# Two token blocks ahead in layer 1's expert stage, and a reordered passage between the layers

## The reference

```python
x = x + tanh(g_xattn) * cross_attention(layernorm(x), ctx)   # 16 heads of 16
x = x + tanh(g_ffn)   * mixture_of_experts(layernorm(x))     # 8 experts, top 2
```

## Time and profile before

| | us |
|---|---|
| median of 3 runs | 691.21 (691.18 to 691.99) |
| the profiled execution | 698.34 |
| its span, first to last instruction | 696.5 |
| PE busy in the span | 641.9 (92%) |
| DVE, ACT, POOL busy | 386.9, 336.9, 268.3 |
| first block of layer 1 starts on PE | 578.85 |
| first and last full block's first product, and first half block's, start | 578.85, 648.02, 650.28 |

### The profile page before, as it was taken

The page is one execution under the profiler, slowest core; times in us unless marked ns, Lnnn a source line. Parts: engine busy times, 40 slices in busy tenths (PEclk is TensorE's granted clock), DMA queues, the critical chain, the costliest instruction groups (busy, mean ns, idle before and its releaser), DMA issues.

```text
span 696.5 us, 18912 instructions
## 1 busy us (share of the span) xinstructions
PE 641.9 (92%) x6536; PEld 506.7 (73%) x6536; DVE 386.9 (56%) x1262; ACT 336.9 (48%) x675; POOL 268.3 (39%) x501
## 2 busy tenths in 40 slices
PE   8899999899999999999999999879999999989960
PEld 5667777667999999999995555557777766768630
DVE  3778899864443322232223222568999896744317
ACT  4566566442455455545531112458777643434420
POOL 5662555533232121112111111214477555866540
PEclk9999999999999999999999999999999999999995
DMA  9144555651123111111115000611122135454219
GB/s 230 38 151 140 165 193 171 207 185 47 62 85 92 39 32 39 36 35 33 39 54 132 32 17 16 209 50 33 62 72 70 63 109 138 148 161 124 81 58 357
DMA packets 50478, 69.74 MB, mean 100 GB/s; under 512 B 7751, under 2 KB 37831, under 8 KB 50387
## 3 DMA queue, kind: packets, MB, share of 16 engines
q1 hardware_dynamic: 41276, 49.66, 23.1%
q0 software_dynamic: 6528, 17.90, 7.2%
q10 hardware_dynamic: 2583, 0.98, 0.6%
HBM read 46.28 MB, written 22.23 MB: 98 GB/s over the span
## 4 chain that ended last, share of the span: by engine, by line
PE 71%; DVE 14%; issue 5%; DMA 5%; POOL 2%; ACT 1%; SPq 1%; another core or an unknown queue 1%; DVEq 0%; POOLq 0%; ACTq 0%
PE ps L1993 17%; PE ps L2049 17%; PE ps L1977 12%; DVE m_rows L1179 4%; PE ps L1763 4%; PE ps L1718 3%; PE ps L1701 3%; PE ps L1755 3%; PE ps L1801 2%; DVE x_sb L1163 2%; PE ps L1777 2%; PE ps L1729 1%; DVE ctx_q L1196 1%; DMA xs_dram<-xn,slot_now 1%; PE ps L2025 1%
## 5 line engine op out<-in xcount | busy, mean ns | idle before, releaser
L2049 PE MATMUL ps<-w_all,share 128*128 (+3 forms) x576 | 137.6, 382 | 3.3 <-ACT w_all L1062 2.1
L718 POOL DMA_INDIRECT ys_dram<-share,dest_i x36 | 37.6, 1044 | 204.1 <-DVE share L1538 203.8
L2049 PEld LDWEIGHTS ps<-w_all,share 128*128 128x128 f32 (+3 forms) x576 | 97.5, 179 | 22.6 <-issue 6.7
L1977 PE MATMUL ps<-w_all,share 128*128 (+1 forms) x336 | 97.5, 430 | 3.8 <-DVE share L1325 3.3
L686 POOL DMA_INDIRECT xs_dram<-xn,slot_now x64 | 66.3, 1036 | 68.0 <-PE ps L1764 15.5
L1993 PEld LDWEIGHTS ps<-share,w_att 128*128 128x128 f32 x768 | 89.4, 192 | 1.3
L1993 PE MATMUL ps<-share,w_att 128*128 128x128 f32 x768 | 89.6, 275 | 0.0
L1977 PEld LDWEIGHTS ps<-w_all,share 128*128 128x128 f32 (+1 forms) x336 | 53.2, 166 | 36.9 <-issue 10.4
L1179 DVE TENSOR_REDUCE m_rows<-ps 128x8 f32<-128x960 f32 x64 | 70.5, 1142 | 12.0 <-PE ps L1718 11.8
L1322 DVE SCALAR_TENSOR_TENSOR xid<-share,be 128x1 f32<-128x1 f32 x36 | 7.8, 217 | 74.8 <-PE ps L1801 60.1
L1011 ACT ACTIVATE share<-ps 128x512 f32<-128x512 f32 x24 | 14.3, 598 | 69.4 <-PE ps L1993 69.4
(11 more groups left out here) (266 smaller groups left out, 1326.0 us busy)
## 6 DMA issues: line engine op xcount, KB each, us to landing
w_all<-ys_dram SPq DMA_DIRECT2D x16, 512.0 KB, 7.1
w_all<-gate SPq DMA_DIRECT2D x8, 688.0 KB
w_all<-up SPq DMA_DIRECT2D x8, 688.0 KB
w_all<-down SPq DMA_DIRECT2D x8, 640.0 KB
w_all<-w SPq DMA_DIRECT2D x16, 256.0 KB
share<-xs_dram SPq DMA_DIRECT2D x28, 129.0 KB
w_all<-xs_dram SPq DMA_DIRECT2D x28, 129.0 KB
out<-x_sb SPq DMA_DIRECT2D x8, 256.0 KB, 5.5
```

Of the source, the lines that this page charges most:

```text
L718: g.indirect_dma_start(ys_dram, bass.IndirectOffsetOnAxis(ap=dest_i[:, w:w + 1], axis=0), block_y(l, j), None).then_inc(stored(l, j)[0], 16)
L1977: i = t.matmul(ps[0:r, bank, 0:w], xgT[:, k, 0:r], w_all[:, bass.ds(off + (k * UPW[l] + col - EW[l]), w)], start=(k == 0), stop=(k == KT - 1))
L2049: i = t.matmul(ps[0:n, 6, 0:D], h[:, 0:n], w_all[0:r, bass.ds(off + (KT * UPW[l] + c * D - EW[l]), D)], start=(c == 0), stop=(c == KD[l] - 1))
```

## The change

1. **Columns two blocks ahead in layer 1.** A second buffer `xgT_odd`; even and odd blocks alternate. At step j PE transposes block j+2 and DVE copies it out, except at step 0 and at steps 11 to 16, where it stays one ahead (`next_blocks`, `REJOIN` = 17). Steps 1 and 17 take two blocks. The transposes still go to bank 7 alone.
2. **Second product three steps behind in layer 1.** Step j does h_t1(j-2) and down(j-3); the last step adds the rest, one pair more than before.
3. **Two result banks in layer 1.** From block 5 on, odd blocks' results go to bank 2, even ones to bank 6, and down(j) waits only for the copy of j-2.
4. **End of layer 0.** h_t0(35) is done in the middle of down(34), into its own column buffer `hT_last`; down(35) writes bank 3; DVE's copy of result 34 comes after the hidden columns of 35; DVE clears 64 rows of `hT_last` once more.
5. **Start of layer 1.** PE's wait for the last result copy moves from ahead of the context transposes to ahead of the values. `v_proj` makes two sequences in the halves of one bank. Between the transpose of sequence 0 and the queries stands only `v_proj` 4; `v_proj` 5 comes after the queries, 6 and 7 as before after the transpose of sequence 1.
6. **The reload of sequence 0** is two DMAs of 256 KB, one for each tile, and `combine` waits for each by itself. This holds after both layers. SP issues 9 DMAs instead of 8.

```diff
         hT = share[:, 1376:2144].rearrange("p (c n) -> p c n", c=6)
+        hT_last = share[:, 2144:2912].rearrange("p (c n) -> p c n", c=6)
         xgT = share[:, 2144:2400].rearrange("p (k n) -> p k n", k=KT)
+        xgT_odd = share[:, 2656:2912].rearrange("p (k n) -> p k n", k=KT)
...
-        BANK_V = (6, 7, 5)
+        BANK_V = ((6, 0), (6, 1), (7, 0), (7, 1), (5, 0), (4, 0), (7, 0), (7, 1))
...
+        TWO_Y = 5
+        def y_bank(l, j):
+            if l == 1:
+                return 2 if j >= TWO_Y and j % 2 else 6
+            return 3 if j == BLOCKS - 1 else 6
+        REJOIN = N1 + 4
+        def next_blocks(j):
+            def ahead(i):
+                return i + 1 if i < 1 or N1 - 2 <= i < REJOIN else i + 2
+            done = ahead(j - 1) if j else 0
+            return [b for b in range(done + 1, ahead(j) + 1) if b < BLOCKS]
...
-                for b in range(NB):
+                for t in range(QT):
+                    sp.dma_start(yg[:, 0, t, :, :].rearrange("p k d -> p (k d)"),
+                                 ys_dram[t * P * TOPK:(t + 1) * P * TOPK, :].rearrange(
+                                     "(p k) d -> p (k d)", k=TOPK)).then_inc(D_first[t], 16)
+                for b in range(1, NB):
...
# ACT, layer 1
-                    if j >= 1:
-                        hT_evac(j - 1)
                     if j >= 2:
-                        y_evac(j - 2)
+                        hT_evac(j - 2)
+                    if j >= 3:
+                        y_evac(j - 3)
...
                     if last:
+                        hT_evac(j - 1)
+                        y_evac(j - 2)
                         hT_evac(j)
                         y_evac(j - 1)
                         y_evac(j)
...
# DVE, combine
                         for t in range(2):
+                            if b == 0 and k == 0:
+                                v.wait_ge(D_first[t], 16 * (L + 1))
...
# DVE, x_evac
-                    need(v, b_up, 4 * j if l == 0 else 4 * BLOCKS + j)
+                    need(v, b_up, 4 * j if l == 0 else 4 * BLOCKS + j - 1)
...
# DVE, layer 0's last step
-                    if not first:
+                    if not first and not last:
                         y_evac(j - 1)
...
                     if last:
+                        y_evac(j - 1)
                         y_evac(j)
...
# DVE, layer 1: x_evac(j + 1) becomes
+                    some_x(next_blocks(j)[:1])
                     v.wait_ge(e_act, 2 * BLOCKS + j + 1)
                     v.wait_ge(b_hT, 2 * OLD0 + j - 1)
                     v.tensor_tensor(h_pair[:, j % 2, :], act_pair[:, j % 2, :], act_pair[:, j % 2, :], ALU.mult).then_inc(e_h, 1)
+                    some_x(next_blocks(j)[1:])
                     beside1(j)
...
# PE, start of layer 1
-                    t.wait_ge(e_y, BLOCKS)
                     ctx_t(0)
...
                     t.wait_ge(L_wv, 32)
+                    t.wait_ge(e_y, BLOCKS)
                     t.wait_ge(C_vz, 1)
-                    for b in range(3):
-                        v_proj(B0 + b, BANK_V[b])
-                    t.wait_ge(d_v, B0 + 1)
-                    v_proj(B0 + 3, BANK_V[0])
+                    v_proj(B0, 6, 2)
+                    v_proj(B0 + 2, 7, 2)
                     t.wait_ge(L_wq, 32)
                     t.wait_ge(a_k, 4 * l + 4)
                     x_t(B0, 2)
-                    t.wait_ge(d_v, B0 + 2)
-                    v_proj(B0 + 4, BANK_V[1])
-                    t.wait_ge(d_v, B0 + 3)
-                    v_proj(B0 + 5, BANK_V[2])
+                    v_proj(B0 + 4, 5)
                     for m in range(KT):
                         q_proj(B0, m, (3, 1)[m])
+                    v_proj(B0 + 5, 4)
                     scores(G0)
-                    t.wait_ge(d_v, B0 + 6)
+                    t.wait_ge(d_v, B0 + 2)
                     x_t(B0 + 1, 6)
-                    v_proj(B0 + 6, 4)
-                    v_proj(B0 + 7, 5)
+                    t.wait_ge(d_v, B0 + 4)
+                    v_proj(B0 + 6, 7, 2)
...
# PE, down
+                    if l == 1 and j >= TWO_Y:
+                        t.wait_ge(e_y, BLOCKS + j - 1)
+                    elif y_bank(l, j) == 6:
+                        need(t, e_y, J0[l] + j)
...
+                        if c == KD[0] // 2 and between is not None:
+                            between()
...
# PE, layer 0's last step
                     if last:
-                        h_t0(j)
+                        down(j - 1, offs[j - 1], lambda: h_t0(j))
                         down(j, offs[j])
...
# PE, layer 1
-                    if not last:
-                        block_t(j + 1)
+                    for n in next_blocks(j)[:1]:
+                        block_t(n)
                     if j == 0:
                         out_proj(G1)
-                    if j >= 1:
-                        h_t1(j - 1)
                     if j >= 2:
-                        down(j - 2, offs[j - 2])
+                        h_t1(j - 2)
+                    if j >= 3:
+                        down(j - 3, offs[j - 3])
+                    for n in next_blocks(j)[1:]:
+                        block_t(n)
...
                     if last:
+                        h_t1(j - 1)
+                        down(j - 2, offs[j - 2])
                         h_t1(j)
                         down(j - 1, offs[j - 1])
                         down(j, offs[j])
```

More of the change, by code:

```diff
@@ L1164, in combine, with values @@
                                                    in1=xt, op0=ALU.mult, op1=ALU.add).then_inc(d_comb if k else d_c1, 1)
[L1166 removed]
+                def values(B, bank, at_=0):
                     b = B % NB
@@ L1356, in _ @@
                 else:
-                    values(B0 + 6, 4)
-                    values(B0 + 7, 5)
+                    for b in range(6, NB):
+                        values(B0 + b, *BANK_V[b])
                 for u in range(NU):
@@ L2034, in h_t1, with down @@
                     i.then_inc(b_hT, 1)
-                def down(j, off):
+                def down(j, off, between=None):
                     if by_weights(l, j):
```

86 lines of the change are left out of this document (47 added, 39 removed).

## The result

The changed kernel takes 693.86 us (median of 7 runs, 693.43 to 694.82), the kernel before 691.38 beside it (7 runs, 690.68 to 692.2). The ratio is 1.0035 (1.0025 to 1.0045): slower by 2.5 us, where 2.4 less was predicted. The profiled execution took 694.1, its span 692.1.

The account below looks back on a forecast made before the run. PE, busy 92% of the span, was taken as the bound, except in the chain between the layers and at the end. Terms (a) to (g) summed to -2.4 off 691.21, giving 688.8 us, range 686.0 to 691.8.

Parts of the forecast that it names:

- (g): Last reload, after layer 1: halves let DVE's first instruction start sooner, -0.4 us (ends -0.9, +0.5).
- (e): Layer 1, steps 13 to 35: two banks remove a wait of down(18) in steps 16 to 20, -0.6 us.
- (a): End of layer 0: block 35's hidden transposes move inside down(34), so its result comes sooner, -0.8 us.
- (b): First reload, after layer 0: halves take one DVE instruction out of the way, -0.4 us (ends -0.9, +0.5).
- (c): Start of layer 1: only one `v_proj` between sequence 0's transpose and the queries, -0.8 us (ends -0.3, -1.1).
- (d): Layer 1, steps 0 to 12: wait for block 13's load grows from 0.67 to about 1.5, +0.2 us.
- (f): Last step of layer 1: three pairs ahead of down(35) instead of two, stores closer together, +0.4 us.
- "Slower": Whole kernel, chance 0.11: lower PE clock at block 13 (697.6 us), or chiefly a stand-still at a new place (694.7).
- The rival "no change": Whole kernel: put-off pair costs its whole 1.1, steps 13 to 35 and reload halves give 0; 691.2 us, chance 0.23.
- The rival that the stand-still goes: Layer 1, steps 12 to 15: reordering removes the idle times of ACT and DVE, 5.9 more; 682.9 us, chance 0.05.

Follow-up runs that it names:

- passage_split: Kernel before with parts 4 to 6 of the change, layer 1's block schedule (parts 1 to 3) undone; 698.94 us, ratio 0.9997.
- split_first_only: Kernel before plus parts 3, 4 and 5, context transposes as late as before, and the reload halved after layer 0 alone; 695.82 us, ratio 0.9967.
- passage_only: Kernel before with parts 4 and 5 of the change alone, blocks and reload as before; 698.67 us, ratio 1.0003.
- after_again: The changed kernel, unaltered, run once more on another occasion; 697.75 us, ratio 0.9986.
- passage_two_banks: Kernel before plus parts 3, 4 and 5, with the wait for the last result copy back ahead of the context transposes; 690.48 us, ratio 0.9976.
- split_third: Kernel before plus parts 3, 4, 5, late context transposes, and sequence 2's load halved in both reloads, sequence 0's whole; 696.71 us, ratio 0.9982.
- lag_only: Kernel before plus parts 2 to 5, late context transposes, columns in two buffers but one block ahead, no split reload; 696.74 us, ratio 0.9980.
- after_last_whole: The changed kernel with the last reload whole again, the one after layer 0 still in halves; 693.55 us, ratio 0.9968.
- blocks_only: Kernel before with parts 1 to 3 of the change alone, passage and reload as before; 693.95 us, ratio 1.0019.

## Why the prediction was wrong

Three things carry the miss. Step (g) took the last reload as 0.4 shorter, and it is 1.9 longer, for the load behind the halves lands late. Step (e) took steps 13 to 35 as 0.6 shorter; they had nothing to give, and steps 0 to 35 are 1.0 to 1.3 longer. And layer 1's attention, put at nothing, took 1.3 more in the profile. Step by step:

*What bounds the kernel.* PE with the passage and the end as exceptions: that held. What did not hold was the basis. I saw that the profiled execution was 7.1 above the median and put the 1.93 and 4.29 aside, but still took steps 16 to 20 and the block-13 passage of that execution for the usual ones.

*(a), predicted -0.8: right.* From block 35's first product to the reload's issue the old end takes 16.08 to 16.37 in four profiles, the new one 15.17 to 15.57 in sixteen (after: 15.25): -0.9.

*(b), predicted -0.4 with ends -0.9 and +0.5: measured -0.6, nearer to the end where each half lands by its own bytes.* In the kernel after the halves land 2.57 and 3.25 behind the first issue, the whole load before 3.79; that the second half lands when the whole did was wrong. From the issue to POOL's first instruction on the statistics, twelve profiles with the first load whole take 6.33 to 6.84, mean 6.56. Eight with halves take 5.64 to 5.76 in six cases (after: 5.65), but 6.39 in passage_split and 7.10 in split_first_only; mean 5.96. In split_first_only the pair's issue took 1.73 instead of 0.84.

*(c), predicted -0.8: right.* 2.19 to 1.32 between transpose and queries, and 0.09 back between queries and scores (3.22 instead of 3.13): -0.8. The step took the queries' start before from the chain, 454.19 for 454.03, so the 0.85 that it read was 0.7. The cover that the step named, PE's wait at 451.84, grew to 2.04 in passage_only, and there the clock fell. In the kernel after the wait is only 0.90, because (b) brings the rows sooner.

*Not in the sum: layer 1's attention, +1.3.* The scores start 2.9 earlier, the first block only 1.6: attention takes 121.73 instead of 120.46. One instruction explains it; timelines of DVE and POOL in the kernel after:

```profile
473.16 1.54 DVE L1241 TENSOR_TENSOR share<-ctx_q,recT 128x256 f32<-128x256 f32 x1
473.15 1.27 POOL L736 TENSOR_TENSOR x_sb<-x_sb,w_all 128x512 f32<-128x512 f32 x1
```

and in after_again, the same code:

```profile
473.15 0.42 DVE L1241 TENSOR_TENSOR share<-ctx_q,recT 128x256 f32<-128x256 f32 x1
473.18 1.52 POOL L736 TENSOR_TENSOR x_sb<-x_sb,w_all 128x512 f32<-128x512 f32 x1
```

Where POOL starts first by 0.01 or 0.02, or in the same hundredth, DVE takes 1.5; where DVE is 0.02 to 0.04 first, it takes 0.42 and POOL 1.52. Of 20 profiles 12 have the slow one, and their attention takes 121.4 to 122.2; the other 8 take 120.4 to 120.9, without exception. The Trainium skill (SBUF — State Buffer, Who interferes with whom) says that a DVE instruction with two inputs in SBUF contends with a GpSimd instruction that reads SBUF, and that the order of issue decides which of the two is blocked; by that rule, the trace agrees, in all 20 profiles. None of the four profiles with the old passage has it. But after_again shows that the code alone doesn't decide it: its attention takes 120.87, only 0.4 more than before. I didn't try to move either instruction, so that keeping them apart gains 1.1 is argued and not shown.

*(d), predicted +0.2: right in its terms.* Block 13's first product comes 32.37 behind block 0's, 32.08 before. The wait grew to 1.25 (1.5 forecast). Against the calm profiles of the old blocks (31.70 to 31.99) it is +0.4 to +0.7.

*(e), predicted -0.6: wrong, the sign.* The excess of 0.77 in steps 16 to 20 was itself a stand-still, which the profile had put down to PE. Of the kernel before:

```profile
631.13 1.03 PE L2049 MATMUL ps<-w_all,share 128*128 x4
632.86 0.38 PE L1801 MATMUL ps<-ident,w_all 128*128 128x128 f32 x2
634.06 0.22 DVE L1322 SCALAR_TENSOR_TENSOR xid<-w_all,be 128x1 f32<-128x1 f32 x1 [2.06 <-PE ps L1801]
```

PE's product was done at 632.16 and ACT's copy of it began at 633.16; the transpose was done at 633.24 and DVE began at 634.06. In the steps before, both begin 0.03 to 0.05 behind PE. In passage_two_banks, with old lag and old columns and no stand-still, these steps take about 2.17 each. There was nothing to win, and the catching up at step 17 costs 0.69, which I hadn't costed at all: the second transpose stands in PE's program ahead of the next first product, which then starts another 0.31 late; the profile doesn't say for what. At step 1 the second transpose waits 0.74 for DVE's copy out of bank 7. Steps 0 to 35 in sum: 83.40 against 82.10 to 82.42, +1.0 to +1.3, where (d) and (e) together had -0.4.

*(f), predicted +0.4: the sign right, the size +0.7, by the stores.* On PE the step held: down(35) starts 5.01 behind the first product of block 35 instead of 4.83, +0.2 where 0.1 was forecast, and without a wait. The last result's copy ends 6.46 behind it instead of 6.33. But POOL issues the last store 1.34 behind that copy instead of 0.78 (668.44 and 667.10; 674.69 and 673.91), because the stores now stand close behind one another on POOL: 0.3 was forecast for that, 0.56 measured. Of the kernel before, the last result's copy:

```profile
673.54 0.37 ACT L1062 COPY w_all<-ps 128x256 f32<-128x256 f32 x1 [1.37 <-PE ps L2054]
```

The term also hides two edits that pull against one another: two banks give 0.8 (8.76 against 9.58), the third pair costs 1.5 (10.28 against 8.76). Kept apart, the answer would have been to take one and leave the other.

*(g), predicted -0.4, end +0.5: wrong, and the largest single error, +1.9.* With halves at the head of the last reload the tail is 20.28 to 22.08 in five profiles, mean 21.0; whole (or split further back) it is 19.11 to 20.23 in fifteen, mean 19.4. I asked when the first instruction starts. It does start 1.05 sooner. But the end is set by all 32, and sequence 1 arrives late. The loads behind the two halves, and those of the kernel before:

```profile
L583 SPq DMA_DIRECT2D w_all<-ys_dram x7: 426/470/1729, 671.8 to 676.2; - x7
DMA to landing us min/median/max: 6.5/9.0/10.6
```

```profile
L549 SPq DMA_DIRECT2D w_all<-ys_dram x8: 391/469/647, 677.2 to 680.9; - x8
DMA to landing us min/median/max: 3.7/7.1/9.8
```

The issues aren't what is slow. The median issue takes 0.47 in both; eight of the nine are out 3.46 behind the first, and only the ninth comes late, at 5.23. What is slow is the landing of the one load right behind the halves. Times from the first issue, read from the trace:

| last reload | issue of sequence 0, 1, 2, 3 | landing of sequence 0, 1, 2, 3 |
|---|---|---|
| before | 0, 0.44, 0.95, 1.46 | 3.72, 5.06, 6.79, 8.16 |
| after | 0 and 0.38, 0.86, 1.33, 1.84 | 2.67 and 3.30, 7.38, 8.68, 10.02 |

Later loads land about 1.35 apart in both. In the other four kernels with halves at the head, sequence 1 lands 5.8 to 8.2 behind the first issue, in the fifteen others 4.9 to 5.2. Those have a smaller pause too, but one load later: sequence 2 lands 1.35 to 2.5 behind sequence 1 (split_third apart), while DVE still has the eight instructions of sequences 0 and 1 to do; only once (lag_only, 2.5) does it leave a gap of over 0.5 and a tail of 20.23. Windows of the fourth to sixth us behind the issue, kernel after (last numbers: granted clock, DMA share, GB/s):

```profile
673.92:674.92 1.00, 0.00 (x0) 0.00 (x0) 0.85 (x3) 0.00 (x0) 0.00 (x0) 0.50 0.51 193
674.92:675.92 1.00, 0.00 (x0) 0.00 (x0) 0.60 (x2) 0.00 (x0) 0.00 (x0) 0.50 0.95 219
675.92:676.92 1.00, 0.00 (x0) 0.00 (x0) 0.00 (x0) 0.00 (x0) 0.00 (x0) 0.50 0.64 244
```

and of the kernel before:

```profile
680.18:681.18 1.00, 0.00 (x0) 0.00 (x0) 0.25 (x1) 0.00 (x0) 0.00 (x0) 0.50 1.05 408
681.18:682.18 1.00, 0.00 (x0) 0.00 (x0) 1.00 (x4) 0.00 (x0) 0.00 (x0) 0.50 0.98 375
682.18:683.18 1.00, 0.00 (x0) 0.00 (x0) 1.00 (x4) 0.00 (x0) 0.00 (x0) 0.50 1.06 404
```

The DMA engines are partly idle (0.51 and 0.64) though seven of the nine loads have been issued by then. After layer 0 the same slowness stays hidden, since there only sequence 0 is urgent. after_last_whole has the tail back at 19.58. Why the load behind two halves lands so late stays open: split_third shows that it isn't the halves alone, and nothing tried separates their place from their size.

*The sum.* Against profiles without a stand-still: (a) -0.9, (b) and (c) -1.7, attention +1.3, steps +1.0 to +1.3, last step +0.7, tail +1.8. That makes +2.2 to +2.5; the medians say +2.5. So close a match is partly luck: the terms come from one profile of the kernel after, and with the short addition, as in after_again, the same sum would be 0.9 lower. How many of the seven runs had the slow one isn't on record.

*The rivals.* "Slower" had 0.11, and neither mechanism of it came: the granted clock of the kernel after stayed at 2.4 GHz from 5.9 to 671.5, past PE's last product, and no stand-still appeared in its profile. The rival "no change" had the right shape, the pair's cost above what it frees. It lacked the tail and the attention. The rival that the stand-still goes was true of the two profiles and worthless for the time. The chance for slower was too small because every term of the passage and the end was taken as a gain with small ends, though the reload had a row (3.79 for 512 KB) for one load only and none for how eight share the engines.

## What to carry to other kernels

Where a whole list of transfers feeds an engine that then runs to the end, look at when the last one or the slowest gap comes and not at when the first lands; split only where one transfer alone is urgent. Cost a larger lag and a second buffer separately: here the second result bank gave 0.8 and the lag took 1.5. And when the profiled execution is 1% above the median, first ask which of its waits are in the median; terms read beside a stand-still are not worth their digits.

## What was unexpected of the hardware

An order of a few hundredths of a us between DVE and POOL decides 1.1 us of the kernel's time, and it falls one way or the other in two executions of the same code (1.54 and 0.42).

A wait of PE of 2.04 was followed by the lower clock, waits of 0.26 to 1.88 at the same place in the other profiles weren't. Yet in blocks_only the clock fell behind waits of 0.55 and 0.34, with which the kernel after kept it.

Two loads of 256 KB ahead of seven of 512 KB cost the last reload 1.6 on average (193 to 244 GB/s for three us instead of 375 to 408), by one late landing and not by slower issues; the same two as third and fourth load cost 0.1.

In four of the five batches DVE and ACT stood still for 1 to 4.3 us at a time between 597 and 636, in every kernel profiled there, mostly near 600, 617 or 633, and the ratio of the changed kernel went from 1.0035 to 0.9986 with it.
